# A two-layer window and pooled attention block with a Winograd convolution: the first image's order and the last image by channel halves

## The reference, cut to what matters

```python
# x: (4, 256, 32, 32)
x = x + attention(_gn(x), ...)          # _gn: group norm over 32 groups
x = x + masked_conv(_gn(x), ...)

# attention, 4 window heads and 4 pooled heads of 32 channels
qkv = xw @ h_qkv_w                      # windows of 2x2 tokens
attn = softmax(q @ k.T * SCALE);  hifi = (attn @ v) @ h_proj_w + h_proj_b
q = xh @ l_q_w;  k, v = split(mean over 2x2 windows of xh @ l_kv_w)
attn = softmax(q @ k.T * SCALE);  lofi = (attn @ v) @ l_proj_w + l_proj_b
out = concatenate([hifi, lofi])         # 1024 queries, 256 pooled keys per image

# masked convolution
mu_x, mu_y = rounded centre of mass of x per channel
m = max(1 - (|posX - mu_x| + |posY - mu_y|) * mask_weight, -1)   where filter == 1, else 1
out = conv3x3(relu(x * m), weight) + bias
```

## Time and profile before

| | |
|---|---|
| median of 3 runs | 425.68 us (424.81 to 427.03) |
| the profiled execution | 424.92 us, of which the span is 423.1 |
| busy: PE, DVE, ACT, POOL | 336.3, 293.3, 114.1, 100.5 us |
| DMA | 20.38 MB, 8611 packets |
| granted clock of PE, mean of the run | 0.883 |

### The profile page before, as it was taken

How to read it: one execution, slowest core, us unless ns; L and a number is a source line. 1 busy time by engine, 2 the same in 40 slices (tenths; PEclk the granted TensorE clock), 3 DMA queues, 4 the chain that set the end, 5 groups by cost and what they waited for, 6 DMA issues and landing times.

```text
span 423.1 us, 4092 instructions
## 1 busy us (share of the span) xinstructions
PE 336.3 (79%) x1544; PEld 237.4 (56%) x1544; DVE 293.3 (69%) x584; ACT 114.1 (27%) x124; POOL 100.5 (24%) x58
## 2 busy tenths in 40 slices
PE   2580967899498599991999599965999999806996
PEld 1360725347374474681868373854877648705885
DVE  4940739877976987887679776896678658885121
ACT  2230014522402536133026243122046300231000
POOL 0288499200083020000910200006600200030000
PEclk9896895799859599997799989995999999965999
DMA  7579300006900000079000400293001001001011
GB/s 243 210 95 155 136 4 0 2 0 84 102 2 3 1 2 1 2 132 104 0 5 0 149 2 0 79 117 42 2 3 50 2 0 52 0 0 50 2 50 50
DMA packets 8611, 20.38 MB, mean 48 GB/s; under 512 B 1680, under 2 KB 4624, under 8 KB 8336
## 3 DMA queue, kind: packets, MB, share of 16 engines
q1 hardware_dynamic: 8592, 20.13, 23.8%
HBM read 7.93 MB, written 4.19 MB: 29 GB/s over the span
## 4 chain that ended last, share of the span: by engine, by line
PE 41%; issue 19%; DVE 16%; DMA 12%; POOL 5%; ACT 3%; SPq 2%; POOLq 0%; DVEq 0%; ACTq 0%
PE slot L838 18%; PE cps L870 17%; DMA ks<-probs 10%; PE cps L838 4%; POOL probs L305 4%; DMA xy<-x 2%; SPq L243 2%; DVE st L488 2%; ACT probs L434 1%; DVE gn L516 1%; POOL mask L297 1%; DVE v_lo L615 1%; PE slot L1008 1%; PE slot L1031 1%; DMA out<-xy 1%
## 5 line engine op out<-in xcount | busy, mean ns | idle before, releaser
L870 PE MATMUL cps<-v_hi,cw_hi 128*128 128x496 f32 (+1 forms) x192 | 79.1, 412 | 19.5 <-DVE xy L670 15.1
L870 PE MATMUL cps<-v_hi,cw_lo 128*128 128x496 f32 (+1 forms) x192 | 78.7, 410 | 0.0
L870 PE MATMUL cps<-v_lo,cw_hi 128*128 128x496 f32 (+1 forms) x192 | 77.8, 405 | 0.0
L305 POOL TENSOR_TENSOR probs<-q_w,k_w 128x1024 f32<-128x1024 f32 x16 | 37.3, 2363 | 139.2 <-DVE rw L583 132.2
L633 DVE TENSOR_REDUCE l_max<-slot 128x4 f32<-128x1024 f32 x32 | 37.7, 1220 | 33.5 <-PE slot L838 33.5
L870 PEld LDWEIGHTS cps<-v_hi,cw_hi 128*128 128x128 f32 x192 | 38.4, 200 | 32.9 <-ACT v_hi L428 20.6
L838 PE MATMUL slot<-ks,qs 96*128 96x256 f32 x128 | 26.5, 362 | 35.6 <-DMA ks<-probs 34.8
L838 PEld LDWEIGHTS slot<-ks,qs 96*128 96x128 f32 x128 | 23.8, 257 | 39.6 <-DMA ks<-probs 36.6
L870 PEld LDWEIGHTS cps<-v_hi,cw_lo 128*128 128x128 f32 x192 | 38.1, 198 | 8.4 <-issue 0.7
L870 PEld LDWEIGHTS cps<-v_lo,cw_hi 128*128 128x128 f32 x192 | 38.2, 199 | 7.1
L434 ACT ACTIVATE probs<-slot 128x1024 f32<-128x1024 f32 x32 | 31.7, 1024 | 36.1 <-PE slot L838 36.0
(11 more groups left out here) (143 smaller groups left out, 545.4 us busy)
## 6 DMA issues: line engine op xcount, KB each, us to landing
qs<-probs SPq DMA_DIRECT2D x12, 512.0 KB, 10.6
xy<-x SPq DMA_DIRECT2D x8, 512.0 KB, 9.2
out<-xy SPq DMA_DIRECT2D x8, 512.0 KB, 2.6
raw_cw<-conv_w SPq DMA_DIRECT2D x2, 1152.0 KB, 7.5
ks<-probs SPq DMA_DIRECT2D x12, 128.0 KB, 13.6
probs<-h_qkv SPq DMA_DIRECT2D x2, 192.0 KB, 4.6
probs<-l_kv SPq DMA_DIRECT2D x2, 128.0 KB, 4.0
probs<-selectors SPq DMA_DIRECT2D x1, 256.0 KB, 4.0
```

The lines of the kernel that those rows point to most:

```text
L305: nc.gpsimd.tensor_tensor(qk[:, j].rearrange("p (n w) -> p n w", n=NW), q_w[:].rearrange("p (n w) -> p n w", n=NW), k_w[:, j * G:(j + 1) * ...
L870: ins = nc.tensor.matmul(cps[:, pos % 2, y0 * WT:y1 * WT], (cw_hi, cw_hi, cw_lo)[part][:, k, pos, dy + 1, o * P:(o + 1) * P], (v_hi, v_lo, ...
```

## The change

In the first image: `w_lo` is made in three pieces, the last two only after the first statistics; the V projection comes right after K's; `window_scores` comes after the transpose of the maxima; of the convolution weights only the first stage of tile 0 stays ahead of the products, and `pv[0] + pv[1]` goes to DVE. In all images: `stack` moves the first 512 queries of each band, then the keys, then the other 512 queries, which count on a semaphore of their own, `stacked_late`; PE waits for it at the fifth block. In the last image: the two channel tiles go through statistics, line sums, mask numbers, masking and the tile operations one after the other (`last_front`), the window output comes ahead of the softmax sums, and the convolution does all eight sums for tile 0, then all eight for tile 1 (`last_convolution`), in eight banks (`last_bank`: the six of the slots and the two of `cps`). Its results are added in `last_result`. The rest of the diff turns helpers into per-tile forms.

```diff
+SPLITS = (slice(WLQ, WLK), slice(WLK, WCOLS), slice(WQ, WLQ))
...
+LAST_ORDER = tuple((o, pos) for phase in range(2) for o in range(KT) for pos in range(2 * phase, 2 * phase + 2))
...
+                def queries(part, parts, half, done):
+                    n = slice(half * HALF, (half + 1) * HALF)
+                    sp.dma_start(qs[HD * part:HD * (part + 1), :, n].bitcast(F32),
+                                 parts[:, n].bitcast(F32)).then_inc(done, 16)
...
                 sp.wait_ge(lq_act, b + 1)
-                rows(qs, 0, lq_hi)
-                rows(qs, 2, lq_hi)
+                queries(0, lq_hi, 0, stacked)
+                queries(2, lq_hi, 0, stacked)
                 sp.wait_ge(lq_dve, b + 1)
-                rows(qs, 1, lq_lo)
+                queries(1, lq_lo, 0, stacked)
                 sp.wait_ge(lk_act, b * 2 + 1)
-                rows(ks, 0, lk_hi)
-                rows(ks, 1, lk_hi)
+                keys(0, lk_hi)
+                keys(1, lk_hi)
                 sp.wait_ge(lk_dve, b + 1)
-                rows(ks, 2, lk_lo)
+                keys(2, lk_lo)
+                for part, parts in enumerate((lq_hi, lq_lo, lq_hi)):
+                    queries(part, parts, 1, stacked_late)
...
@@ -346,20 +363,29 @@
                 wait_count(pool, mask_c, b * N_MASK)
                 products(b)
                 if first:
-                    conv_weights(1)
+                    conv_weights(0, 1)
+                    conv_weights(1, 0)
+                    conv_weights(1, 1)
                 else:
                     mask_sum(b - 1, b + 1)
-                pool.wait_ge(pv_ready, b * NW + 2)
-                nc.gpsimd.tensor_tensor(pv[0], pv[0], pv[1], ALU.add).then_inc(pv_pool, 1)
+                    pool.wait_ge(pv_ready, b * NW + 2)
+                    nc.gpsimd.tensor_tensor(pv[0], pv[0], pv[1], ALU.add).then_inc(pv_pool, 1)
...
             pool.wait_ge(w_split, 1)
-            nc.gpsimd.tensor_tensor(w_lo[:], raw_w, w_hi[:].bitcast(F32), ALU.subtract).then_inc(w_split, 1)
-            pool.wait_ge(w_split, 2)
+            for i, cols in enumerate(SPLITS):
+                if i == 1:
+                    pool.wait_ge(gn_c[0], N_GN)
+                nc.gpsimd.tensor_tensor(w_lo[:, :, cols], raw_w[:, :, cols], w_hi[:, :, cols].bitcast(F32),
+                                        ALU.subtract).then_inc(w_split, 1)
+            pool.wait_ge(w_split, 1 + len(SPLITS))
             pool.wait_ge(pool_c, N_POOL)
-            conv_weights(0)
+            pool.wait_ge(cw_in, KT * 16)
+            conv_weights(0, 0)
...
+            for k in range(KT):
+                pool.wait_ge(mask_last[k], N_MASK)
+                mask_sum_of(k)
...
+                if first:
+                    nc.vector.tensor_tensor(pv[0], pv[0], pv[1], ALU.add).then_inc(pv_pool, 1)
...
+                if last:
+                    residual(b, 0, 1)
+                    dve.wait_ge(y_ready, B * KT - 1)
+                    half[0].of_channels()
...
-                residual(b, 0, 1)
+                if not last:
+                    residual(b, 0, 1)
...
+                if last:
+                    half[0].of_groups()
+                    half[0].scale_and_bias()
+                    residual(b, 1, 2)
+                    last_front()
+                    return
...
+            half = [Statistics(B - 1, 1, range(k, k + 1), gn_last[k], gn_last_pe[k], k + 1) for k in range(KT)]
+            def last_front():
+                b, older = B - 1, B - 2
+                dve.wait_ge(y_ready, B * KT)
+                half[1].of_channels()
+                conv_result(older, (V_LEFT, V_RIGHT))
+                line_sums(b, slice(0, 1), mask_last[0])
+                mask_parts(b, slice(0, 1), mask_last[0])
+                conv_result(older, (POS + V_SUM,))
+                half[1].of_groups()
+                half[1].scale_and_bias()
+                masked_image(b, 0)
+                conv_result(older, (POS + V_DIFF,))
+                conv_tiles(b, 0, 0)
+                line_sums(b, slice(1, 2), mask_last[1])
+                conv_low(b, 0, 0)
+                conv_tiles(b, 0, 1)
+                conv_result(older, (POS + V_LEFT, POS + V_RIGHT))
+                conv_low(b, 0, 1)
+                mask_parts(b, slice(1, 2), mask_last[1])
+                masked_image(b, 1)
+                for phase in range(2):
+                    conv_tiles(b, 1, phase)
+                    conv_low(b, 1, phase)
...
+                    if pos == V_SUM:
+                        ins = nc.vector.scalar_tensor_tensor(y, m.unsqueeze(1).to_broadcast([P, 2, HALF]),
+                                                             cbias[:, o:o + 1], y, ALU.add, ALU.add)
+                    else:
+                        before = V_SUM if pos == V_DIFF else V_DIFF
+                        dve.wait_ge(conv_out, done + LAST_ORDER.index((o, before)) + 1)
+                        for side in ((0, 1), (0,), (1,))[pos - 1]:
+                            ins = nc.vector.scalar_tensor_tensor(y[:, side], m, (1.0, -1.0)[side], y[:, side],
+                                                                 ALU.mult, ALU.add)
...
-            mask_parts(B - 1)
-            for k in range(KT):
-                masked_image(B - 1, k)
-            for k in range(KT):
-                conv_tiles(B - 1, k, 0)
-            for k in range(KT):
-                conv_low(B - 1, k, 0)
-            for k in range(KT):
-                conv_tiles(B - 1, k, 1)
-            conv_result(B - 2, (POS + V_LEFT, POS + V_RIGHT))
-            for k in range(KT):
-                conv_low(B - 1, k, 1)
-            conv_result(B - 1, range(EVENTS))
+            last_result()
...
+            def group_means_of(k):
+                pe.wait_ge(gn_last[k], GN_SENT)
+                mm(slot[k + 1][:, 0, 0:2], cst[:, C_GRP:C_GRP + P], mv[1][:, k], True, True).then_inc(gn_last_pe[k], 1)
+            def last_convolution(k):
+                done = (B - 1) * EVENTS
+                for i, (o, pos) in enumerate(LAST_ORDER):
+                    if i % POS == 0:
+                        pe.wait_ge(v_act, (B - 1) * POS + k * 2 + pos // 2 + 1)
+                        pe.wait_ge(v_dve, (B - 1) * POS + k * 2 + pos // 2 + 1)
+                    if k == 0 and (o, pos) == (1, V_SUM):
+                        pe.wait_ge(conv_out, done)
+                    if k == 0 and pos == V_LEFT:
+                        pe.wait_ge(gn_last[o], GN_SENT + 1)
+                    for m in range(POS_MM // KT):
+                        row, part = divmod(m, 3)
+                        dy = ROW_ORDER[k][row]
+                        y0, y1 = max(0, -dy), min(H, H - dy)
+                        ins = nc.tensor.matmul(last_bank(o, pos)[:, y0 * WT:y1 * WT],
+                                               (cw_hi, cw_hi, cw_lo)[part][:, k, pos, dy + 1, o * P:(o + 1) * P],
+                                               (v_hi, v_lo, v_hi)[part][:, k, pos, (y0 + dy) * WT:(y1 + dy) * WT],
+                                               start=k == 0 and m == 0, stop=k == KT - 1 and m == POS_MM // KT - 1)
...
+                    if k == KT - 1:
+                        ins.then_inc(conv_pe, 1)
...
+                if first:
+                    pe.wait_ge(w_split, 3)
...
-                if not first:
+                if first:
+                    pe.wait_ge(w_split, 4)
+                else:
...
+                else:
+                    project(cps, WV)
...
+                    if n == NB // 2:
+                        pe.wait_ge(stacked_late, (b + 1) * STACK_LATE)
...
-                    if first and n == 2:
-                        project(cps, WV)
...
-                if not first:
-                    window_scores(b, slot[0])
+                if first:
+                    pe.wait_ge(qkv_sb, 3)
+                window_scores(b, cps if first else slot[0])
...
                 pe.wait_ge(st_exp, (b + 1) * LT)
+                if last:
+                    window_out()
                 by_head(2, lambda t, h: cst[:, C_ONE:C_ONE + HD], lden_pe)
...
+                if not last:
+                    window_out()
                 by_head(0, lambda t, h: lv[:, t, HD * h:HD * (h + 1)], lpv_pe)
+                if last:
+                    pe.wait_ge(y_ready, B * KT - 1)
+                    group_means_of(0)
...
+            for k in range(KT):
+                last_convolution(k)
```

218 lines of the change are left out of this document (124 added, 94 removed).

## The result

The changed kernel takes 395.16 us (median of 4 runs, 394.12 to 396.05), the kernel before 425.59 beside it: a ratio of 0.928 (95% interval 0.925 to 0.931), 30.4 us less. The forecast was 394.1 us, range 386 to 403. The profiled run took 395.26 us (span 393.4).

| up to | before | after | stretch before | stretch after | difference | forecast |
|---|---|---|---|---|---|---|
| first queries | 23.05 | 23.26 | 23.05 | 23.26 | +0.2 | -1.0 |
| second image's queries | 98.13 | 89.51 | 75.08 | 66.25 | -8.8 | -6.4 |
| third image's | 182.83 | 173.79 | 84.70 | 84.28 | -0.4 | 0 |
| fourth image's | 272.52 | 259.97 | 89.69 | 86.18 | -3.5 | -5.1 |
| last image's `k_w` | 345.78 | 328.34 | 73.26 | 68.37 | -4.9 | -6.0 |

The account below looks back on a forecast made before the run. It took a DMA queue to bound each image's start, and a DVE chain then 35.30 us of matmuls the end. From 424.92 us, 7.4 + 0 + 5.1 + 6.0 + 12.3 = 30.8 came off, giving 394.1 us, range 386 to 403.

Parts of the forecast that it names:

- Stacking, price per byte: Query and key transfers: time goes by bytes, so the early part lands 6.8 us sooner, the late part when all lands now.
- halves without effect: Rival on stacking: engines serve all nine transfers in turns, the early part lands with the late; 408.6 us, chance 0.03.
- a charge by the row: Rival on stacking: the queue charges by row, each half takes as long as a whole; 434 us, chance 0.01.
- The start, 1.0 us: First image: low parts of the weights in three pieces end the statistics sooner; 1.0 us taken, between 0.2 and 2.8.
- Window sums, 9.4 us: First image: with halves and early V projection the window sums end 9.4 us sooner, 8.2 to 10.5.
- 2 us given back (0 to 5.5): First image: DVE's additions and statistics come sooner and wait beside POOL's weights; 2 us lost, 0 to 5.5.
- First image, 7.4 us: Term for the whole first image: 9.4 us gained less 2 lost; bounds 4 and 11.
- second rival: First image: POOL and DVE block each other and alternate, 5.5 instead of 2 lost; 397.6 us, chance 0.22 with first rival.
- First rival, the clock: First image: PE idles, the clock stays at 1.2 GHz, 5 us lost; 399 us, chance 0.22 together with the second rival.
- the forecast's signs of being wrong: Unchanged `ks<-probs` wait; clock 0.5 between 45 and 70; DVE additions of 2 us or more; gap in the last convolution.
- Third and fourth, 5.1 and 6.0: Third and fourth images: early queries let DVE's eight maxima run back to back; 5.1 us (3 to 5.1) and 6.0 (3.5 to 6.1).
- Last image, 12.3: Last image: tile by tile, the convolution starts at 374.8 instead of 384.06 and runs faster; 12.3 us, bounds 8 and 14.

Follow-up runs that it names:

- whole pieces: The changed kernel with one transfer for each query piece, then the keys, no late half: ratio 0.958 to the kernel before, 12.6 us lost.
- Kept high: The changed kernel with warming matmuls in PE's waits of the first image: ratio 0.924 to the kernel before, 1.6 us gained, unresolved.
- POOL out of the way: The changed kernel with the first image's warming matmuls and POOL's last four weight instructions held until the second image's statistics: 0.917, 391.5 us.
- With the waits filled: The changed kernel with convolution matmuls moved ahead of and between the third and fourth images' score blocks: ratio 0.933 to the kernel before, 2.0 us lost.
- the half-filled start: The changed kernel with eight instead of five warming matmuls ahead of the first projection: ratio 0.924 to the kernel before, 1.8 us gained, unresolved.

## Why the prediction was right, and where it was not

- **Stacking, price per byte: right.** Early part 6.6 us sooner (6.8 said), late part at 41.0 (40.5 said), whole pieces 41.01. The rivals of halves without effect and of a charge by the row are refuted by the same rows.
- **The start, 1.0 us: mis-sized.** In the changed kernel's trace it is -0.2, on average over eight traces with that start some 0.2. The stall of 3.27 us shrank and the statistics ended 2.7 us sooner, as said; the other two pieces stretched DVE's first two normalisations to 3.55 us instead of 1.00, also said. In this trace PE's last warming matmul was over at 13.5, the clock fell at 15.6 instead of 17.7, and the first projection lost in speed what it had gained in start (0.67 us). The step left the clock out.
- **Window sums, 9.4 us: 8.4**, at the lower end of the 8.2 to 10.5 that the two clocks gave.
- **2 us given back (0 to 5.5): mis-sized; on net nothing was.** From the end of the window sums to the next queries it takes 39.3 us before and 39.1 after. The rows blocked by POOL at the additions and statistics do lose 5.5 us, and POOL is held up too, so the second rival's mechanism is shown; but of its 5.5 us, meant for the additions, these lose 2.3 and two rows of the statistics 3.2. The sum had left out the other side. The same weights had before stood beside the softmax, whose three last rows took 4.7 us and now 1.9, so that DVE's loss beside POOL grew only from 4.4 to 7.2 us from there on. And two waits of DVE for PE are gone, which in the kernel before are these:

```profile
84.29 0.72 DVE L775 STREAM_TRANSPOSE v_w<-slot 128x512 f32<-128x512 f32 x1 [1.00 <-PE slot L838]
...
89.85 1.22 DVE L782 TENSOR_TENSOR k_w<-slot,v_w 128x1024 f32<-128x1024 f32 x1 [1.63 <-PE slot L838]
```

  From the softmax's fifth instruction to `k_w` the stretch grew only from 26.9 to 27.7.
- **First image, 7.4 us: 8.6 by this trace, and partly luck.** In the three other traces that run the whole first image unchanged the second image's queries are issued at 90.16, 91.65 and 92.14, not at 89.51: 8.0, 6.5 and 6.0 us sooner than before, with the 8.6 on average 7.3. There is one such trace of the kernel before.
- **First rival, the clock: half right.** It is 0.50 from 36 to 50 and from 57 to 67, as that rival said, but its price of 5 us was not paid on top; that the waits of DVE beside POOL hid it is argued from the traces. Kept high, it gave 1.6 us alone, unresolved, and 4.6 with POOL out of the way. Two of the forecast's signs of being wrong came true (a clock of 0.50 between 45 and 70, an addition of over 2 us on DVE) and the time was right all the same.
- **Second image 0: right** (0.4).
- **Third and fourth, 5.1 and 6.0: mis-sized, 3.5 and 4.9.** The failing term is "PE needs 1.6 us per block with its five convolution matmuls", read at full clock; after its waits PE took 2.2 and 2.6, mostly at 0.50. With the waits filled, the eight maxima and the result took 9.8 us, where the sum had assumed 9.9.
- **Last image, 12.3: 12.3 by the trace, 11.9 by undoing it.** Start of the convolution 28.1 us behind `k_w` (29.0 said), PE idle 1.7 us before it (3 at most), full clock, a bank in 4.04 us, no gap between the tiles, all as written.
- By the two traces the total was 1.1 us off because the surplus of the first image (1.2) and of the second (0.4) makes up for part of the 2.7 that the third and fourth lacked.

## What to carry over

When a wait gets shorter, read the clock of the work behind it: after a gap of two to three microseconds the next blocks often ran at half clock here. Filling some of the gaps did not help in a way that the runs resolve (1.6 us with 2.1 uncertain); it did together with moving POOL's work (4.6 us with 2.2 uncertain). Of work that is moved on POOL, count both where it will stop DVE and where it no longer does, and place it beside DVE's instructions that read PSUM, its statistics or its reductions. One input alone is no protection: a cast and the first image's normalisation (`xn<-xy,gn`), each with one wide SBUF tensor, were held up too (1.73 us for 0.23, 3.55 for 1.00). Two costs that cover one another, as POOL's and the clock's seem to here, each look cheap when removed alone. And before a single trace is believed to a microsecond, look for the same stretch in traces of other kernels that leave it unchanged.

## What the runs showed that was not expected

- The clock often fell in the middle of dense work and not in the gap before it: in the changed kernel PE idles from 32.9 to 34.8 at 1.00, works from 34.8 on, and drops to 0.50 at 36.1; in the third image it idles from 183.3 to 185.3 and drops at 186.3. Other falls lie in the gap itself, as the one at 15.6 (idle from 13.5 to 16.7).
- Once low it stayed so for 6.9 us (15.6 to 22.5, PE at work from 16.7 on) and, with the half-filled start, for 10.3 us (18.4 to 28.7, PE at work from 19.2 on).
- A tiny DVE instruction can cost it a whole one of POOL's: two of 0.15 us took 1.80 and 1.76 beside low parts, which take POOL 1.81 undisturbed. Reads of PSUM (1.23), statistics (0.62 each) and reductions of one tensor ran at their normal length beside the same weights.
- Runs of one kernel differ by up to 4.5 us (392.9 to 397.4).
